# Linear attention on one core: norms with token halves in rows of their own, factors among the last queries, three buffers of scaled queries, their low halves by VectorE

## The reference

```python
q = hidden_states @ Wq.T + bq
k = hidden_states @ Wk.T + bk
v = hidden_states @ Wv.T + bv
...
sq = elu_plus_one(q)          # 16 heads of 128
sk = elu_plus_one(k)          # 4 groups of 128, each for 4 heads
kv = jnp.einsum('bhsd,bhse->bhde', sk, v)
qkv = jnp.einsum('bhsd,bhde->bhse', sq, kv)
k_sum = sk.sum(axis=2)
norm = jnp.einsum('bhsd,bhd->bhs', sq, k_sum)
attn = qkv / (norm[..., None] + EPS)
...
return attn @ Wo.T
```

## Time and profile before

| | us |
|---|---|
| median of 3 runs | 839.14 |
| the runs | 835.45, 839.14, 839.41 |
| the profiled execution | 842.74 |
| its span, first to last instruction | 840.7 |
| phase 1 in it, four batches | 11 to 361 |

### The profile page before, as it was taken

One profiled execution on the slowest core, in us unless ns is written; L12 is line 12 of the kernel. 1 busy time (PEld: TensorE's weight loads), 2 busy tenths in 40 slices (PEclk: granted clock), 3 DMA queues, 4 the chain that ended last, 5 costly groups with the idle time before them and its releaser, 6 DMA issues.

```text
span 840.7 us, 10896 instructions
## 1 busy us (share of the span) xinstructions
PE 723.7 (86%) x3836; PEld 486.0 (58%) x3836; DVE 528.6 (63%) x1135; ACT 410.0 (49%) x742; POOL 106.4 (13%) x102
## 2 busy tenths in 40 slices
PE   4798999889989998934678998899999999999764
PEld 3667886778768776833433453355555545455454
DVE  3568556855586558553365777777978787762243
ACT  3474347434754465421202674576556665556422
POOL 0301320132013301315000100010002000000000
PEclk9999999999999999975755896899999999879968
DMA  9200000010000100010650182028100840000000
GB/s 350 76 1 0 27 0 1 1 40 0 0 0 0 69 0 0 0 47 1 75 75 2 23 102 29 2 38 95 23 2 17 93 70 2 1 2 27 26 0 26
DMA packets 13588, 28.22 MB, mean 34 GB/s; under 512 B 2593, under 2 KB 3433, under 8 KB 13033
## 3 DMA queue, kind: packets, MB, share of 16 engines
q1 hardware_dynamic: 13544, 27.67, 17.6%
HBM read 12.59 MB, written 2.10 MB: 17 GB/s over the span
## 4 chain that ended last, share of the span: by engine, by line
PE 39%; DVE 10%; ACT 3%; issue 2%; DMA 2%; POOL 1%; SPq 0%; ACTq 0%; POOLq 0%; DVEq 0%
PE bank_st L1012 8%; PE bank_c L1025 6%; DVE nmax L1512 5%; PE side L962 4%; PE side L1083 3%; PE bank_s L993 3%; PE side L1114 2%; PE side L1043 2%; PE side L945 1%; DMA ks<-qk_lo 1%; PE side L914 1%; PE side L976 1%; ACT xk L1249 1%; DVE ln_bn L1470 1%; PE bank_t L1033 1%
## 5 line engine op out<-in xcount | busy, mean ns | idle before, releaser
L1512 DVE TENSOR_REDUCE nmax<-bank_s 128x1 f32<-128x512 f32 x256 | 164.8, 685 | 75.6 <-PE bank_s L993 74.8
L1293 ACT ACTIVATE shared<-bank_st 128x512 f32<-128x512 f32 x256 | 139.1, 596 | 78.2 <-PE bank_st L1012 77.4
L993 PE MATMUL bank_s<-ks,qs 48*128 48x512 f32 x256 | 117.6, 526 | 19.4 <-DVE nmax L1512 11.6
L1012 PE MATMUL bank_st<-qs,ks 50*128 50x512 f32 x256 | 106.2, 487 | 8.3 <-ACT shared L1293 4.7
L361 PE MATMUL bank_y<-m_hi,s_lo 128*128 128x256 f32 x256 | 75.4, 294 | 16.4 <-ACT s_hi L468 8.4
L522 DVE SCALAR_TENSOR_TENSOR sq<-bank_q,bq,eq 128x512 f32<-128x512 f32 x64 | 46.6, 738 | 51.3 <-ACT eq L428 51.3
L468 ACT ACTIVATE s_hi<-sq 128x512 fp32r<-128x512 f32 x64 | 40.4, 631 | 78.8 <-PE bank_y L361 66.1
L1025 PE MATMUL bank_c<-shared,v 128*32 128x512 f32 x512 | 76.9, 676 | 0.9 <-ACT shared L1293 0.9
L1012 PEld LDWEIGHTS bank_st<-qs,ks 50*128 50x128 f32 x256 | 43.2, 201 | 57.3 <-issue 32.1
L361 PE MATMUL bank_y<-m_lo,s_hi 128*128 128x256 f32 x256 | 73.9, 288 | 0.0
L361 PE MATMUL bank_y<-m_hi,s_hi 128*128 128x256 f32 x256 | 73.7, 288 | 0.0
(11 more groups left out here) (242 smaller groups left out, 1353.2 us busy)
## 6 DMA issues: line engine op xcount, KB each, us to landing
qs<-qk_hi SPq DMA_DIRECT2D x16, 256.0 KB, 5.5
ks<-qk_hi SPq DMA_DIRECT2D x16, 256.0 KB, 10.0
xT<-in_xT SPq DMA_DIRECT2D x4, 512.0 KB, 5.1
sq<-in_wqT SPq DMA_DIRECT2D x2, 1024.0 KB, 9.0
wo<-in_woT SPq DMA_DIRECT2D x1, 2048.0 KB, 12.6
xs<-in_x SPq DMA_DIRECT2D x1, 2048.0 KB, 17.5
qs<-qk_lo SPq DMA_DIRECT2D x8, 256.0 KB, 7.8
ks<-qk_lo SPq DMA_DIRECT2D x8, 256.0 KB, 10.5
```

What stands on the lines that cost most here:

```text
L993: pe.matmul(bank_s[u % 2][:, :], qs[part, b % 2, slot, t * P:(t + 1) * P], ks[part, b % 2, slot, :], start=True, stop=True).then_inc(s_don ...
L1012: pe.matmul(bank_st[u % 2][:, :], ks[part, b % 2, slot, kt * P:(kt + 1) * P], qs[part, b % 2, slot, :], start=True, stop=True).then_inc(st ...
L1293: act.activation(probs[:, u % SLOTS, :], bank_st[u % 2][:, :], ACT.Exp, scale=SCALE1).then_inc(p_ready, 1)
L1512: dve.tensor_reduce(nmax[:, g, t, j:j + 1], bank_s[u % 2][:, :], AX.X, ALU.max, negate=True).then_inc(max_ready, 1)
```

## The change

The tokens of a head are cut into two halves in `norm`: row 2(j mod 2)+q of a group's 32 rows gets token half q of head j. One norm is now eight products of 256 columns instead of four of 512, and `bank_n`'s first 256 columns hold heads 0 to 7, the others heads 8 to 15. `den`, `rn`, `rn_c` and `rn_parts` are 256 wide, so the epsilon, the reciprocal, `factor_hi` and `parts` each run once on 256 columns for eight heads. `factor` is two products of 256 columns with two columns of `pick`.

Factors 0 to 2 move among queries 13 to 15, projections 0 to 2 as well, and a list `USES` gives the order in which queries and factors take the three banks; the one that takes a bank waits for what last emptied it. The first three norms and the third and fourth output map stand earlier or later than before, so that a norm follows its heads at more distance; the last norm stands after project 2. `s_hi` and `s_lo` get three buffers, all low halves are made by DVE, one head behind the scaling, and POOL has none. `split_x` runs in two pieces of 512 columns, between heads 8 and 12. The statistics of the residual are spread over queries 3, 5 and 7.

The core of the diff (the prologue, the waits' base counts and the pick tables on the host follow from it):

```diff
+HALVES = 2
+TH = T // HALVES
+USES = ([("query", n) for n in range(13)] + [("factor", 0), ("query", 13), ("factor", 1), ("query", 14), ("factor", 2), ("query", 15)]
+        + [("factor", n) for n in range(3, H0)])
+USE = {use: k for k, use in enumerate(USES)}
...
-        pick_raw, pick = sb("pick_raw", [H0]), sb("pick", [H0], F32R)
+        pick_raw, pick = sb("pick_raw", [H0 * HALVES]), sb("pick", [H0 * HALVES], F32R)
...
-        ksel = sb("ksel", [G0, J0, 32])
+        ksel = sb("ksel", [G0, 2 * HALVES, 32])
...
-        den, rn = sb("den", [T]), sb("rn", [T])
-        rn_c, rn_parts = sb("rn_c", [T], F32R), sb("rn_parts", [2, T], F32R)
+        den, rn = sb("den", [TH]), sb("rn", [TH])
+        rn_c, rn_parts = sb("rn_c", [TH], F32R), sb("rn_parts", [2, TH], F32R)
         m_hi, m_lo = sb("m_hi", [4, 2 * D], F32R), sb("m_lo", [4, 2 * D], F32R)
-        s_hi, s_lo = sb("s_hi", [2, T], F32R), sb("s_lo", [2, T], F32R)
+        s_hi, s_lo = sb("s_hi", [3, T], F32R), sb("s_lo", [3, T], F32R)
...
-        MAP_AT = (4, 6, 14, 15)
+        MAP_AT = (4, 6, 8, 11)
+        def q_bank(kind, n):
+            return bank_q[USE[kind, n] % 3]
...
-            def scaled_lo(b, n):
-                pool.wait_ge(s_hi_ready, H0 * b + n + 1)
-                at_least(pool, s_lo_ready[1], H0 // 2 * b + n // 2)
-                pool.tensor_tensor(s_lo[:, 1, :], sq[:, n, :], s_hi[:, 1, :].bitcast(F32), ALU.subtract).then_inc(s_lo_ready[1], 1)
...
+            def q_bank_free(b, kind, n):
+                k = USE[kind, n]
+                if k < 3:
+                    at_least(pe, scaled, H0 * b)
+                elif USES[k - 3][0] == "query":
+                    pe.wait_ge(sq_ready, H0 * b + USES[k - 3][1] + 1)
+                else:
+                    pe.wait_ge(scaled, H0 * b + USES[k - 3][1] + 1)
...
-                    mm = pe.matmul(bank_n[32 * g:32 * g + 32, :], ksel[:, g, j, :], sq[:, G0 * j + g, :],
-                                   start=j % 2 == 0, stop=j % 2 == 1)
+                for q in range(HALVES):
+                    tok = slice(q * TH, (q + 1) * TH)
+                    for g in range(G0):
+                        mm = pe.matmul(bank_n[32 * g:32 * g + 32, (j // 2) * TH:(j // 2 + 1) * TH], ksel[:, g, HALVES * (j % 2) + q, :],
+                                       sq[:, G0 * j + g, tok], start=j % 2 == 0 and q == 0, stop=j % 2 == 1 and q == HALVES - 1)
...
-                pe.matmul(bank_q[(H0 + n) % 3][:, :], pick[:, h:h + 1].broadcast_to([P, P]), rn_parts[:, n // (H0 // 2), :],
-                          start=True, stop=True).then_inc(bc_done, 1)
+                q_bank_free(b, "factor", n)
+                for q in range(HALVES):
+                    mm = pe.matmul(q_bank("factor", n)[:, q * TH:(q + 1) * TH], pick[:, HALVES * h + q:HALVES * h + q + 1].broadcast_to([P, P]),
+                                   rn_parts[:, n // (H0 // 2), :], start=True, stop=True)
+                mm.then_inc(bc_done, 1)
...
-                for n in range(3, H0):
+                for n in range(3, 13):
                     query(b, n)
                     if n in MAP_AT:
                         output_map(b, MAP_AT.index(n))
-                    if n % G0 == 1 and n > G0:
-                        norm(b, n // G0 - 1)
+                    if n in (6, 9):
+                        norm(b, n // 3 - 2)
                 pe.wait_ge(setup_done, 4)
                 factor(b, 0)
+                query(b, 13)
+                norm(b, 2)
                 factor(b, 1)
-                norm(b, J0 - 1)
-                for n in range(H0):
+                query(b, 14)
+                project(b, 0)
+                factor(b, 2)
+                query(b, 15)
+                factor(b, 3)
+                project(b, 1)
+                factor(b, 4)
+                project(b, 2)
+                norm(b, 3)
+                for n in range(3, H0):
...
+            def scaled_hi(b, n):
+                act.wait_ge(scaled, H0 * b + n + 1)
+                at_least(act, y_done, H0 * b + max(0, n - 2))
+                act.activation(s_hi[:, n % 3, :], sq[:, n, :], ACT.Copy).then_inc(s_hi_ready, 1)
...
+                    if n == 10:
+                        factor_hi(b, 0)
                     if n in MAP_AT:
                         map_hi(b, MAP_AT.index(n))
-                    if n == PARTS_AT + 3:
-                        factor_hi(b, 0)
-                for n in range(H0):
+                    if n in (12, 13, 14):
+                        scaled_hi(b, n - 12)
+                for n in range(3, H0):
+                    scaled_hi(b, n)
                     if n == 4:
                         factor_hi(b, 1)
-                    act.wait_ge(scaled, H0 * b + n + 1)
-                    at_least(act, y_done, H0 * b + max(0, n - 1))
-                    act.activation(s_hi[:, n % 2, :], sq[:, n, :], ACT.Copy).then_inc(s_hi_ready, 1)
-                    if n in (3, 5, 7, 9):
-                        map_hi(b, 4 + (n - 3) // 2)
-                    if n == 10 and more:
-                        split_x(b + 1)
+                    if n in (5, 7, 9, 11):
+                        map_hi(b, 4 + (n - 5) // 2)
+                    if n in (8, 10) and more:
+                        split_x(b + 1, (n - 8) // 2)
...
-            def invert_tokens(b, half_, i):
+                dve.tensor_scalar(den[:, :], bank_n[:, half_ * TH:(half_ + 1) * TH], DEN_EPS, None, ALU.add).then_inc(den_ready, 1)
                 dve.wait_ge(den_ready, 2 * b + half_ + 1)
-                tok = slice(i * T // 2, (i + 1) * T // 2)
-                dve.reciprocal(rn[:, tok], den[:, tok]).then_inc(rn_ready, 1)
+                dve.reciprocal(rn[:, :], den[:, :]).then_inc(rn_ready, 1)
...
-                        invert_tokens(b, 1, n - 1)
+                scale(b, 0)
+                query(b, 12)
+                scaled_lo(b, 0)
+                scale(b, 1)
+                query(b, 13)
+                scaled_lo(b, 1)
+                query(b, 14)
+                scale(b, 2)
+                scaled_lo(b, 2)
+                query(b, 15)
+                scale(b, 3)
+                scale(b, 4)
+                scaled_lo(b, 3)
+                invert(b, 1)
+                scaled_lo(b, 4)
+                for n in range(5, H0):
+                    scale(b, n)
                     if n == 5:
                         parts(b, 1)
-                    if n in (4, 6, 8, 10):
-                        map_lo(b, 4 + (n - 4) // 2)
-                    if n == 12 and more:
-                        split_x(b + 1)
+                    if n > 5:
+                        scaled_lo(b, n - 1)
+                    if n in (6, 8, 10, 12):
+                        map_lo(b, 4 + (n - 6) // 2)
+                    if n in (9, 11) and more:
+                        split_x(b + 1, (n - 9) // 2)
+                scaled_lo(b, H0 - 1)
```

More of the change, by code:

```diff
@@ L302, in query @@
                     for lhs, rhs in split_passes(wq_hi[:, k, hd], wq_lo[:, k, hd], xT_hi[:, k, :], xT_lo[:, k, :]):
-                        mm = pe.matmul(bank_q[n % 3][:, :], lhs, rhs, start=i == 0, stop=i == 3 * KD - 1)
+                        mm = pe.matmul(q_bank("query", n)[:, :], lhs, rhs, start=i == 0, stop=i == 3 * KD - 1)
                         i += 1
@@ L358, in project @@
                     tok = slice(t * P, (t + 1) * P)
-                    for i, (lhs, rhs) in enumerate(split_passes(s_hi[:, n % 2, tok], s_lo[:, n % 2, tok], m_hi[:, m, cols], m_lo[:, m, cols])):
+                    for i, (lhs, rhs) in enumerate(split_passes(s_hi[:, n % 3, tok], s_lo[:, n % 3, tok], m_hi[:, m, cols], m_lo[:, m, cols])):
                         mm = pe.matmul(bank_y4[:, t, :], lhs, rhs,
@@ L574, in body @@
                 at_least(dve, s_hi_ready, H0 * b)
-                for i in range(2):
-                    at_least(dve, s_lo_ready[i], H0 // 2 * b)
+                at_least(dve, s_lo_ready, H0 * b)
                 for n in range(3):
@@ L622, in _ @@
             residual(B - 1)
-            residual_stats(B - 1)
+            residual_stats(B - 1, range(NT))
+            residual_merge(B - 1)
 def by_tile(x):
@@ L1795, in constants @@
         for j in range(J0):
-            pick[32 * g + j, J0 * g + j] = pick[32 * g + 4 + j, J0 * g + j] = 1.0
-            part_c[32 * g + j], part_c[32 * g + 4 + j], part_m[32 * g + 4 + j] = 1.0, -1.0, 1.0
+            for q in range(HALVES):
+                row, col = 32 * g + HALVES * (j % 2) + q, HALVES * (J0 * g + j) + q
+                pick[row, col] = pick[row + 16, col] = 1.0
+                part_c[row], part_c[row + 16], part_m[row + 16] = 1.0, -1.0, 1.0
     return {"pick": pick, "part_c": part_c, "part_m": part_m, "ones": np.ones((P, 1), np.float32),
```

92 lines of the change are left out of this document (38 added, 54 removed).

## The result

The changed kernel takes 813.89 us (median of 4 runs, 813.18 to 819.37); the kernel before, with one more run beside it, 837.30 (4 runs, 833.33 to 839.41). The ratio is 0.974, 95% interval 0.9681 to 0.98: faster by 2.6%. On a second chip it was 0.9762 (0.9714 to 0.981). The forecast was 816, range 808 to 827.

A forecast was written before the change was run, and what follows sets the result against it. PE was taken to bound phase 1, by its work plus gaps. A ceiling of 30.7 us less 2.4 of added work and 5.6 of new waits gave 22.7 us, from 839.1 to 816 us, range 808 to 827.

The forecast's parts named there:

- The ceiling: PE's gaps in phase 1: at most 30.7 us can go, from listed waits, modelled ends and lower clock.
- hidden by modelled ends: PE's 24 waits in phase 1: each gap is about 0.17 us longer than listed, 4.1 us in all.
- The clock's term: First projections of three batches: run at the lower clock after a wait, 1.3 us lost each, 3.9 us.
- The added work: PE's norms and factors: more product starts cost 0.4 and 0.2 us a batch, 2.4 us in all.
- Rival C: Norms: row parts run one behind the other at 256 columns, 48 us more, 864 us; chance 0.05.
- The new waits: PE before query 13 and the projections behind the second reciprocal: 1.4 us a batch, 5.6 us in all.
- DVE's saving from the halves: DVE per batch: 3.5 us of reciprocals and 1.3 us on four other instructions saved, 4.8 us.
- the one on length: Sign in the profile after: each batch of phase 1 lasts 79 to 80.5 us.
- the one on the third buffer and DVE's low halves: Projections: two heads of lead give 3.3 us for a 2.8 us chain, so the waits on POOL go.
- rival B: DVE becomes late: heads 5 to 15 lose 0.2 us each, 8.8 us more, 825 us; chance 0.13.
- Rival D: Gaps move into queries 12 to 15, 7.7 us of new waits a batch, no change, 839 us; chance 0.06.
- Rival E: Clock behind phase 1: later phases' clock may fall at other points, 3 us either way; no chance of its own.

The follow-up runs named there:

- DVE's order at the second reciprocal: Changed kernel with the low half of head 4 and scaling of head 5 ahead of DVE's second reciprocal: 813.67 us, ratio 0.9684.
- the two-buffer variant: Changed kernel with two buffers of `s_hi` and `s_lo` instead of three: 814.35 us, ratio 0.9667.
- norms later: Kernel before with its first three norms one query later, nothing else: 839.29 us, ratio 0.9985.
- the variant with three buffers: Kernel before with three buffers of `s_hi` and `s_lo` and all low halves by DVE: 838.68 us, ratio 0.9954.

## Why the prediction was right

**The ceiling.** Gaps of 22.7 us listed, 4.1 hidden by modelled ends and 3.9 of lower clock made 30.7. Of the listed gaps 19.2 us are gone (22.7 less the 3.5 that are left or new). The measured 22.7 us leave 3.5 us for the other two terms, where the ceiling had 8.0. The clock's term was nearly right: the second and third batch went from 0.98 to 1.00, 2% of 86 us each, 3.4 us; the first shows 0.96 in both kernels, because the changed one lost the fall near 71 us and had a longer one near 30 us. That leaves nothing for the hidden ends, the term that was mis-sized in the sum. The single experiments do not agree on it: where listed waits of 10.5 us came back, so did 10.5 us, but where 1.8 us of them went (DVE's order at the second reciprocal) 3.2 us were gained. What a hidden end is worth stays open.

**The added work** was forecast at 0.6 us a batch and is not there: a norm lasts 1.07 us as before, its next query starts 1.00 us behind it. A factor's two products take the 0.23 us of the one. Rival C is out by the same row. By the about 60 cycles that the Trainium skill (TensorEngine Tiling (Array Packing), Instruction Overhead) puts on each matmul, an estimate of 25 ns, the 48 starts more would have been 1.2 us a batch. The trace does not agree: a norm of sixteen listed instructions takes the 1.07 us of one of eight.

**The new waits** were walked out at three places, and the chip shows them there. (1) Query 13 on the sq of query 11: forecast 0.5 us; the factor ahead starts at 219.56 and the query at 220.38, 0.82 apart where a factor takes 0.23:

```profile
219.56 0.40 PE L350 MATMUL bank_q<-rn_parts,pick 128*128 128x256 f32 x2
220.38 0.50 PE L308 MATMUL bank_q<-xT_hi,wq_lo 128*128 128x512 f32 x1 [0.42 <-DVE sq L544]
```

That is 0.6 us. (2) Projection 4 behind the second reciprocal: forecast 0.4, measured 0.1 (its factor starts at 234.66, it starts at 235.19, 0.53 apart where 0.43 follows a map). (3) Projection 5: forecast 0.5, measured 0.5. On DVE, from the second epsilon on, the low half of head 5 is the last row here:

```profile
232.34 0.42 DVE L566 TENSOR_SCALAR den<-bank_n 128x256 f32<-128x256 f32 x1
232.79 1.75 DVE L568 RECIPROCAL rn<-den 128x256 f32<-128x256 f32 x1
234.46 0.63 DVE L555 TENSOR_TENSOR s_lo<-sq,s_hi 128x512 fp32r<-128x512 f32 x1
235.01 0.67 DVE L561 TENSOR_TENSOR sq<-sq,bank_q 128x512 f32<-128x512 f32 x1
235.60 0.48 DVE L573 SCALAR_TENSOR_TENSOR rn_parts<-rn,part_m,rn_c 128x256 fp32r<-128x256 f32 x1
236.00 0.68 DVE L561 TENSOR_TENSOR sq<-sq,bank_q 128x512 f32<-128x512 f32 x1
236.59 0.68 DVE L555 TENSOR_TENSOR s_lo<-sq,s_hi 128x512 fp32r<-128x512 f32 x1
```

and PE, whose projection 5 is held up:

```profile
237.42 0.35 PE L367 MATMUL bank_y<-m_hi,s_lo 128*128 128x256 f32 x1 [0.33 <-ACT s_hi L449]
```

It starts 0.83 us behind that low half; ACT's copy is named and was not the last. Taking the reciprocal out of this row of work gave 3.2 us, more than the 2.4 us that (2) and (3) show.

**The sum** came out at 22.7 us for phase 1 and 22.7 us were measured there. That is better than its terms deserve, and the match is luck: the ceiling was 4.5 us too high, and so were the added costs, 8.0 us forecast against the 3.5 us of waits. The clock near 30 us, which the prediction does not have, may have taken up to 0.9 us off the gain (the difference of the two-buffer variant from the changed kernel). The median was helped by luck as well: 816 was counted from 839.1 us, with the fourth run the kernel before stands at 837.3, and three of the four changed runs had the higher mean clock. Two smaller readings were off. DVE's saving from the halves, 4.8 us a batch, measured 4.0 (its four other instructions save 0.28 us each by the earlier trace rows, 1.1 together and not 1.3). And of the signs the one on length missed for the first batch: it takes 88.9 us, not 79 to 80.5.

**The parts.** Undone or done alone, in the end of phase 1: halves 3.2 us, norms later 2.9, buffers with DVE's low halves 4.9, the interleaving (taken off the changed kernel) 10.5; 21.5 us together, each of the first three uncertain by 1 or 2 us of the clock's, so that the nearness to 22.7 shows little. The step that was wrong in its mechanism is the one on the third buffer and DVE's low halves, which it priced as one edit: in the changed kernel each is enough alone. In the order of before DVE's low halves alone gave as much as both; the third buffer alone was not run there. The margin of 0.3 us in two heads that it gave DVE is why rival B had 0.13. With POOL helping, the last three batches took the same 231.1 us, so B's pressure does not show.

**Rival D** (the gaps move into queries 12 to 15) is there with 0.6 us a batch, before query 13, of the 7.7 that the prediction says it needs (28.3 us over four batches are 7.1: the added work was already taken off). **Rival E** was named and left without a chance of its own. It is real: 6 us between two executions of one kernel, twice the 3 us put on it, though not caused by the change.

## What to carry to other kernels

Where PE waits for a chain over three engines, count the PE work that lies between the chain's start and its use, and put work there that does not hang on it; moving a piece from one side of another piece within that stretch changes nothing. Before adding a buffer and a faster engine for the same wait, undo each alone: a chain that is too long by 0.5 us needs only one of them. A long instruction such as a reciprocal belongs behind the short ones in its queue that someone waits for soon.

## What the runs showed of the hardware

The work behind phase 1 is the same in all variants. In five profiles it takes 472.5 to 474.2 us at a mean granted clock of 0.85, in nine 478.3 to 484.2 at 0.83 or 0.84 (in the changed kernel PE is busy 396 or 403 us in it). The repeated kernel's six runs on one chip have both levels of total time, 813.7 us at 0.911 and 819.8 to 823.4 at 0.895 to 0.901. Why an execution takes the one or the other was not found; it sets a floor of 6 us and more under single comparisons, while the last three batches of phase 1 repeated to 0.1 us.

Sixteen products on four row parts of 256 columns take the same 1.07 us as eight of 512 (1.09 us with the parts' products in the other order).

The lower clock did not follow every wait of one length: before, the wait of 1.78 us ahead of the first projection led to 0.50 in the third batch, and the wait of 1.78 us at the same place of the fourth did not. In the variant with three buffers a wait of 1.81 us at the same place of the last batch was followed by products 0.12 us apart, the upper level:

```profile
324.16 0.35 PE L350 MATMUL bank_y<-m_hi,s_lo 128*128 128x256 f32 x1 [1.81 <-ACT s_hi L457]
324.35 0.28 PE L350 MATMUL bank_y<-m_lo,s_hi 128*128 128x256 f32 x1
324.47 0.28 PE L350 MATMUL bank_y<-m_hi,s_hi 128*128 128x256 f32 x1
```

A low half of 512 columns took POOL 1.27 to 1.31 us in the kernel before, but 2.33 and 2.34 us in the two of its 32 that ran beside DVE's 1.22 us for 1024 columns of x. With the split of x in two pieces no low half by POOL took over 1.61 us.
